# First expert's weight remainders, tile turning and gate scaling moved in a two-block attention and expert kernel

## The reference

```python
# attention, 16 heads of width 16; q and k through softplus and a rotation
q, k, v = x @ wq.T, x @ wk.T, x @ wv.T
scores = q_embed @ k_embed.T / sqrt(16)
x = layernorm(x + softmax(scores) @ v @ wo.T)
# experts: 8, the best 2 of each token, at most 640 slots for each expert
gates = softmax(x @ router_w + router_b)
mask = one_hot(top_k(gates, 2)).sum(1)
pos = cumsum(mask, axis=0) - 1            # the slot; at 640 and over it is dropped
buf[e, pos] = x                           # dispatch
out = gelu(buf @ w1[e] + b1[e]) @ w2[e] + b2[e]
y = sum over e of gates[:, e] * out[e, pos] * valid
x = layernorm(x + y)
```

## Time and profile before

| | |
|---|---|
| time, median of 3 runs | 961.52 us (957.97 to 962.7) |
| the profiled execution | 961.35 us, span of its core 959.6 us |
| TensorE busy | 909.4 us (95%) |
| ScalarE busy | 729.2 us (76%) |
| VectorE busy | 622.3 us (65%) |
| GpSimd busy | 456.4 us (48%) |
| mean granted TensorE clock | 0.98 |
| attention block | to about 702 us |
| expert block | from 702.2 us on |

### The profile page before, as it was taken

One profiled execution on the slowest core, in us unless ns is written; L12 is line 12 of the kernel. 1 busy time (PEld: TensorE's weight loads), 2 busy tenths in 40 slices (PEclk: granted clock), 3 DMA queues, 4 the chain that ended last, 5 costly groups with the idle time before them and its releaser, 6 DMA issues. The chain is left out here.

```text
span 959.6 us, 19180 instructions
## 1 busy us (share of the span) xinstructions
PE 909.4 (95%) x7249; PEld 498.6 (52%) x7249; DVE 622.3 (65%) x1202; ACT 729.2 (76%) x889; POOL 456.4 (48%) x382
## 2 busy tenths in 40 slices
PE   8799999999989999998999999999579999999994
PEld 6333343344334334333333433334469999998993
DVE  5665446447785655777555577537737878888776
ACT  6588978887777899786789879987235887778873
POOL 0274225144364645526574454522614557566674
PEclk9999999999999999999999999999789999999998
DMA  7769442343534245353433524531263455534411
GB/s 220 237 224 343 149 156 76 118 143 133 192 133 161 105 135 188 111 187 118 156 109 108 186 95 168 169 107 36 80 210 113 123 180 177 164 116 142 140 59 56
DMA packets 62200, 139.73 MB, mean 146 GB/s; under 512 B 10242, under 2 KB 31299, under 8 KB 61584
## 3 DMA queue, kind: packets, MB, share of 16 engines
q1 hardware_dynamic: 41040, 74.46, 23.8%
q0 software_dynamic: 21056, 63.93, 18.8%
HBM read 71.43 MB, written 66.54 MB: 144 GB/s over the span
## 5 line engine op out<-in xcount | busy, mean ns | idle before, releaser
L689 ACT ACTIVATE prob<-spsum 128x1024 f32<-128x1024 f32 x512 | 493.1, 1022 | 112.3 <-PE spsum L881 103.3
L905 PE MATMUL opsum<-prob,val 128*17 128x512 f32 x2048 | 272.7, 602 | 1.3 <-DVE oraw L1271 0.4
L881 PE MATMUL spsum<-area_q 32*128 32x512 f32 x1536 | 133.1, 427 | 4.8 <-DMA area_q<-aT 3.1
L881 PE MATMUL spsum<-stacks 32*128 32x512 f32 x1536 | 134.7, 426 | 1.5 <-ACT prob L689 1.5
L881 PEld LDWEIGHTS spsum<-area_q 32*128 32x128 f32 x1536 | 72.9, 184 | 118.9 <-ACT prob L689 62.8
L881 PEld LDWEIGHTS spsum<-stacks 32*128 32x128 f32 x1536 | 73.9, 183 | 115.4 <-ACT prob L689 62.5
L1279 DVE RECIPROCAL oden<-oden 128x256 f32<-128x256 f32 x62 | 108.7, 1753 | 2.1
L574 POOL TENSOR_TENSOR onorm<-oraw,oden 128x512 f32<-128x512 f32 x31 | 41.7, 1345 | 120.8 <-DVE oden L1279 116.0
L517 POOL TENSOR_TENSOR square<-raw 128x512 bf16<-128x512 f32 x28 | 53.7, 1919 | 81.2 <-DVE raw L1077 81.1
L519 POOL TENSOR_TENSOR area_s<-emb,area_s 128x1024 fp32r<-128x1024 f32 x28 | 66.5, 2376 | 52.2 <-DVE area_s L1097 52.2
L533 POOL DMA_INDIRECT dispatched<-res,scatter_idx x64 | 66.2, 1034 | 50.3 <-issue 27.4
(11 more groups left out here) (217 smaller groups left out, 1286.4 us busy)
## 6 DMA issues: line engine op xcount, KB each, us to landing
split_scratch<-area_s POOLq DMA_DIRECT2D x60, 512.0 KB, 4.8
area_k<-in_w SPq DMA_DIRECT2D x16, 1024.0 KB, 7.4
stacks<-split_scratch SPq DMA_DIRECT2D x28, 512.0 KB, 5.0
area_q<-split_scratch SPq DMA_DIRECT2D x28, 512.0 KB
dispatched<-blank POOLq DMA_DIRECT2D x1, 5300.0 KB, 25.8
rows<-dispatched SPq DMA_DIRECT2D x7, 662.5 KB
res<-in_x SPq DMA_DIRECT2D x4, 1024.0 KB, 8.4
aT<-onorm SPq DMA_DIRECT2D x124, 32.0 KB
```

The source lines that it names most:

```text
L689: act.activation(prob[u % NPB][:], spsum[u % NSB][:].rearrange("p a n -> p (a n)"), ACT.Exp, scale=HD ** -0.5).then_inc(s_exp, 1)
L881: ins = pe.matmul(spsum[u % NSB][:, j % 2, :], kst[par][rows, a, P * kt:P * (kt + 1)], qst[par][rows, b, cols], start=i == 0, stop=i == 2 ...
L905: ins = pe.matmul(opsum[32 * j:32 * j + HD + 1, :], val[b % 2][:, kt, h0 + j, :], prob[(2 * s + j // 2) % NPB][:, HALF * (j % 2):HALF * (j ...
```

## The change

Three parts. In the attention block VectorE's four subtractions for expert 0's weights are gone; VectorE makes them in the expert block, the two for w1 first, then (behind the five tiles) the two for w2. A new semaphore `s_first_lo` counts them. TensorE waits for it ahead of expert 0's first layer (2) and second layer (4), and SyncE ahead of loading expert 1's w1 (2) and w2 (4), since these loads write over the raw weights. Second, expert 0's five tiles are turned into five banks in place of two, and ScalarE copies their high parts, VectorE only subtracts. Third, the gates of each unit are normalised by a function of their own (`gates`) that is called before VectorE waits for the `place` products.

```diff
@@ attention, vector: read_out
+                if kind == "place":
+                    gates(c)
                 dve.wait_ge(s_full, number[job] + 1)
@@ attention, vector: slots
-            def slots(u, pos):
+            def gates(u):
...
                 link(dve.reciprocal(rs[:, 2, T], rs[:, 1, T]))
                 link(dve.tensor_tensor(ress[b % 2][:, T, GATES:GATES + EXPERTS], rt[:, 0, T], wide(rs[:, 2, T], n),
                                        ALU.mult))
+
+            def slots(u, pos):
+
+                b, t0, t1 = UNITS[u]
+                T, n = slice(t0, t1), t1 - t0
@@ attention, vector: end
             second_scale(BATCH - 1)
-            for n, (raw_w, parts_w) in enumerate(((raw1, w1s), (raw2, w2s))):
-                dve.wait_ge(s_whi, n + 1)
-                rows = raw_w.shape[1] // 2
-                for part in (slice(0, rows), slice(rows, 2 * rows)):
-                    dve.tensor_tensor(parts_w[:, 1, part], raw_w[:, part], parts_w[:, 0, part].bitcast(F32),
-                                      ALU.subtract)
@@ experts
+        s_first_lo = sem("s_first_lo")
...
+        def turned_bank(n):
+
+            return (tp[0][:], tp[1][:], yp[0][:], yp[1][:], hp[1][:, 0])[n] if n < ST else tp[n % 2][:]
@@ experts, sync: load_weights
                     sp.wait_ge(s_w1lo, KC * (e - 1))
+                else:
+                    sp.wait_ge(s_first_lo, KC)
                 sp.dma_start(raw1, w1_d[e].rearrange("(k p) n -> p k n", p=P)).then_inc(s_w1, 16)
                 if e >= 2:
 
                     sp.wait_ge(s_w2lo, KC * (e - 1))
+                else:
+                    sp.wait_ge(s_first_lo, 2 * KC)
                 sp.dma_start(raw2, w2_d[e].rearrange("(k p) n -> p k n", p=P)).then_inc(s_w2, 16)
@@ experts, tensor: turn
-                if n >= 2:
+                if e and n >= 2:
                     pe.wait_ge(s_turned, n - 1)
                 for k in range(KC):
-                    ins = pe.transpose(tp[n % 2][:, P * k:P * (k + 1)],
+                    ins = pe.transpose(turned_bank(n)[:, P * k:P * (k + 1)],
                                        rows[e % 2][:, t, P * k:P * (k + 1)], ident[:])
@@ experts, tensor: ahead of the first and of the second layer
                     pe.wait_ge(s_w1lo, KC * e)
+                else:
+                    pe.wait_ge(s_first_lo, KC)
...
                     pe.wait_ge(s_w2lo, KC * e)
+                else:
+                    pe.wait_ge(s_first_lo, 2 * KC)
@@ experts, scalar
             act.preload_act_table(ACT.Gelu)
+            for t in range(ST):
+                turned_high(0, t)
             act.wait_ge(s_b1, 16)
@@ experts, vector: turned
-                if e == 0:
-                    dve.tensor_copy(hi, src).then_inc(s_xhi, 1)
@@ experts, vector
+            def first_remainders(raw_w, parts_w):
+
+                rows = raw_w.shape[1] // KC
+                for part in (slice(rows * k, rows * (k + 1)) for k in range(KC)):
+                    dve.tensor_tensor(parts_w[:, 1, part], raw_w[:, part], parts_w[:, 0, part].bitcast(F32),
+                                      ALU.subtract).then_inc(s_first_lo, 1)
+
+            first_remainders(raw1, w1s[0])
             for t in range(ST):
                 turned(0, t)
+            first_remainders(raw2, w2s[0])
```

More of the change, by code:

```diff
@@ L1585, in turned_high @@
                 act.copy(xe[e % 2][:, 0, :, P * t:P * (t + 1)],
-                         tp[n % 2][:, 0:DIM].rearrange("p (k n) -> p k n", k=KC)).then_inc(s_xhi, 1)
+                         turned_bank(n)[:, 0:DIM].rearrange("p (k n) -> p k n", k=KC)).then_inc(s_xhi, 1)
             def rstd_guess(n, e, T):
@@ L1656, in turned @@
                 dve.wait_ge(s_turn, n + 1)
-                src = tp[n % 2][:, 0:DIM].rearrange("p (k n) -> p k n", k=KC)
+                src = turned_bank(n)[:, 0:DIM].rearrange("p (k n) -> p k n", k=KC)
                 hi, lo = (xe[e % 2][:, i, :, P * t:P * (t + 1)] for i in range(2))
-                if e == 0:
-                    dve.tensor_copy(hi, src).then_inc(s_xhi, 1)
                 dve.wait_ge(s_xhi, n + 1)
```

## The result

The changed kernel takes 954.86 us in the median of 9 runs (951.69 to 957.59), the kernel before 959.17 us in 9 runs beside it (956.06 to 963.44). The ratio is 0.995 (0.9927 to 0.9973). Run once more later, beside 31 runs of before, the ratio was 0.9944 (0.9923 to 0.9965). The change makes the kernel 0.5% faster, by 4.3 us in these medians and by 5.3 in the later ones. The profiled execution took 957.59 us, with a span of 955.8 us against 959.6.

The account below looks back on a forecast made before the run. TensorE was taken to bound the kernel, so only its standstill or slow running counted. Gates 0.50, scatters 2.0 and turning 2.8 sum to 5.3 us: 961.5 - 5.3 = 956.2 us, range 954.4 to 959.4.

Parts of the forecast that it names:

- The seam: End of attention block: gates ahead of the wait gain 0.50 us, subtractions moved out free GpSimd's scatters for 2.0 us.
- Beside a subtraction: Last eight scatters: the two lying mostly beside VectorE's subtractions take 1.99 and 1.97 us, others 0.98; removal gains 2.0 us.
- Behind the last scatter: From GpSimd's last scatter to the second block, where rows land and engines meet: 3.2 us, kept unchanged.
- Rival (e): Part of the gain is given back, at TensorE's end of the seam or in the first expert: 959 us, chance 0.09.
- The turning: Start of expert block: five banks and two engines bring the fifth tile to S + 6.4, first products to S + 5.5; gain 2.8 us.
- rival (c): Expert block: turning too comes early, after a warm-up at full clock; gain 5.8 to 6.5, about 955.3 us, chance 0.08.
- this low spell: TensorE granted 0.5 (1.2 GHz) from 708.9 to 711.9 on the first products, 12 taking 3.5 us; forecast not to return.
- rival (a): Low clock falls on the first products again, GELU near S + 9.1: gain 3.6, 957.9 us, chance 0.17.
- the third term of the sum: Turning the first expert's tiles in five banks by two engines, with no low clock: 2.8 us, bounds 1.1 and 3.3.
- The waits on SyncE's queue: Expert block: loads of the second expert's w1 and w2 wait for the subtraction pairs; b2 has 1.6 us slack, cost 0.
- the slower rival: Wait for the second pair delays b2 and stops VectorE; 0.5% slower, about 967 us, if b2 takes 23 us; chance 0.04.
- 0.48 for "faster": Whole kernel: chance of measuring faster past the 0.5% bound, 956.7 us; slower 0.04, the rest 0.48.

Follow-up runs that it names:

- the doubled run: Kernel before with its four attention-block subtractions made twice, the first round each waiting for completion; the eight scatters took 11.96 us, one run.
- 12 idle products: Changed kernel with 12 idle TensorE products at the start of the expert block in place of 8; ratio to before 0.9952 (0.9931 to 0.9972).
- two queues: Changed kernel with loads of the first expert's tiles 1 and 3 issued from ScalarE's queue, the others from SyncE's; 959.35 us, ratio to before 0.9969.
- PSUM as an input: Changed kernel plus four back-to-back VectorE instructions at the subtractions' old place, second input from PSUM; mask to end 270.5 us, one run.

## Why the prediction was right or wrong

**The seam.** Right, step by step: 0.50 us for the gates and 2.0 us for the scatters, in the changed kernel and in each part alone. The reason given for the scatters was too coarse. "Beside a subtraction" fits neither the first scatter, which the forecast itself named as speaking against it, nor the doubled run; slow scatters came only beside queued instructions with two SBUF inputs and no gap, and not all scatters beside such a queue were slow. What the forecast took from the Trainium skill's inference ("SBUF — State Buffer", "Who interferes with whom"), that a tensor_tensor shouldn't hold up GpSimd's DMAs, doesn't hold in this case: the scatters took 1.99 and 1.97 us beside two SBUF inputs, and all eight took 0.98 with a PSUM input. Whether it is the writing of descriptors that is held, or the scatter's reading of its index, no run here tells apart. The same section of the Trainium skill also says that an instruction with two SBUF inputs contends with a GpSimd instruction that reads SBUF, and these runs agree with it: the scatter reads `scatter_idx` from SBUF. The full block for the whole instruction, which that section of the Trainium skill states for VectorE's 2-port modes, isn't what these subtractions show: the single ones with waits cost a scatter nothing.

**Behind the last scatter.** The forecast kept the 3.2 us. They were 2.4 us, and in the other traces from 1.7 to 3.1; among the kernels that leave the subtractions where they were it was 3.1 with the gates alone and 2.45 with the turning alone. So 0.75 us of this trace's gain is in a term that varies by itself. In the changed kernel's trace the semaphore record has TensorE arriving at the meeting at 699.71, GpSimd done with its waits at 699.35. Rival (e)'s first half was there, at a third of a microsecond: TensorE took 2.1 us from its last idle product to the meeting, and the forecast had put it at up to 2.9 without loss.

**The turning.** Right in its times. The third tile, the fifth tile and the start of the first products are at S + 5.4, 6.5 and 5.55, forecast 5.5, 6.4 and 5.5. What was left out: with the warm-up at full clock the rows' landing becomes the wait, which kept rival (c) from coming, and the first GELU starts 0.4 us behind the last product's issue, so that S + 7.35 was never to be had. With no low spell it was S + 8.0, a gain of 2.1 us for the 2.8 taken.

**The clock.** This is the step that failed. "I take it that this low spell doesn't come back": it came back in the profiled execution, and the first GELU stood at S + 9.1 as rival (a) had it. In the two traces of the changed kernel it came once, and in three variants with its turning (12 idle products, two queues, PSUM as an input) it fell on the first products as well. With PSUM as an input the clock had already fallen during the warm-up; in the other two it fell behind the turnings. So the third term of the sum, 2.8 us, measured 1.1, and 2.1 in the trace without a low spell.

The reason given for the 2.8 us was that the sparse stretch gets a microsecond shorter. It didn't: from the end of the warm-up to the first product it was 3.13 us before, and 3.51 and 3.48 us in the two traces of the changed kernel, because the warm-up ended 1.4 us sooner and the first product only 1.0. It was hardly denser either (1.74 of 3.10 us busy beside 1.66 of 3.20). The forecast kept the two parts of the change apart, and the traces suggest that they meet here. In the five traces in which TensorE stood still 4.9 us or more ahead of the warm-up, the warm-up was granted 0.5 for all or most of its length; in seven in which it stood still 2.1 to 2.5 us, it was granted 1.0; in one more at 2.5 us and in one at 2.8 the clock fell during the warm-up. With the turning alone the seam was long, the warm-up slow, and the stretch behind it 2.28 us, a microsecond shorter as forecast; its first products were granted 1.0. No run changed the standstill by itself, so this link isn't shown.

Taking the term as 1.1 to 2.1 us, as both traces have it, the sum is 3.6 to 4.6, and with what varied behind the last scatter and behind the first GELU 4.8 to 5.6.

**The waits on SyncE's queue.** No cost, as forecast. b2 was issued at 709.24 and took 8.9 us where the forecast kept 11.0; VectorE read it first at 723.67, 5.5 us later. With a slack of 5.5 us and not 1.6, the slower rival was farther off than put.

**The number.** 956.2 us forecast, 954.86 measured, and within the range. That it came so near is luck in part: the kernel before was itself 2.35 us faster in the nine runs than in the three that the forecast started from, and the gain was 1.0 us smaller than forecast; the two errors have opposite signs. Within the gain, 0.75 us behind the last scatter and 0.5 behind the first GELU, which no term of the sum stands for, made up for most of what the clock took. As a difference, 5.3 us were forecast, 4.3 measured in the medians of these runs and 5.3 in the second set. The ratios 0.995 and 0.9944 lie at the 0.5% bound or just past it, as the forecast put it, and both intervals exclude no change: on the direction the rows were surer than the 0.48 for "faster" said. The upper end of the range is a small slip: 958.2 and 1 us are 959.2, not 959.4.

## What to carry to other kernels

When GpSimd sends the last transfers ahead of a meeting of all engines, look at what VectorE does beside them: a queue of instructions with two SBUF inputs cost 2 us here, and moving them, reading one input from PSUM, or a wait between them each gave it back (the last two in one trace each). Compare small changes over the stretch that they touch, between two marks of the trace, and not over the whole run, when an untouched block alone differs by several microseconds between executions. And when you take waits out of a stretch in which TensorE is sparsely busy, count on the clock's low level on what follows until a trace shows otherwise; filling the pauses with idle products kept the clock up here and gained nothing, in part since they stood in the way of the work. And when two parts of a change meet at one place, work out what the first does to the premise of the second.

## What the hardware showed that was not expected

A wait for completion between two VectorE subtractions of 1.22 us is enough for GpSimd's scatters to keep to 0.98 us each; VectorE's pairs then take 2.49 and 2.54 us for 2.36 and 2.35. Four such subtractions without waits made two scatters take 1.96 to 1.99 us in four traces, and eight with one wait made three, while one scatter that lay wholly beside them took 0.98. The loads of five tiles from one queue landed in 3.1 and 2.8 us in the median in two traces, and from two queues in 3.5 and 4.1 us in one. The warm-up at the start of the second block ran at a granted clock of 1.0 in seven traces in which TensorE had stood still for 2.1 to 2.5 us before it, and at 0.5 to 0.57 in the five in which it had stood still for 4.9 us or more; in two others, at 2.5 and 2.8 us, the clock fell on the way.
